# Attention and gated layer of four batches on one core: unit orders replaced, eleven zero products removed, first-batch products reordered, down projection in two units a bank

## The reference

```
xn = layernorm(x)
s  = causal_attention(xn; 16 heads of 16) @ Wo.T
W  = (wq - 128) * scale[:, None]            # for gate, up and down
g  = silu( (silu(xn @ Wgate.T) * (xn @ Wup.T)) @ Wdown.T )   # hidden size 704
out = x + s * g
```

## Time and profile before

| what | value |
|---|---|
| median of 3 runs | 287.1 us (285.98 to 288.08) |
| the profiled execution's own time | 287.32 us |
| its span, first to last instruction | 285.6 us |
| mean granted TensorE clock | 0.994 |
| PE busy | 272.3 us, 95% of the span |
| PEld / DVE / ACT / POOL busy | 202.0 / 209.5 / 174.0 / 133.1 us |

### The profile page before, as it was taken

How to read it: one execution, slowest core, us unless ns; L and a number is a source line. 1 busy time by engine, 2 the same in 40 slices (tenths; PEclk the granted TensorE clock), 3 DMA queues, 4 the chain that set the end, 5 groups by cost and what they waited for, 6 DMA issues and landing times.

```text
span 285.6 us, 5873 instructions
## 1 busy us (share of the span) xinstructions
PE 272.3 (95%) x2088; PEld 202.0 (71%) x2088; DVE 209.5 (73%) x722; ACT 174.0 (61%) x258; POOL 133.1 (47%) x235
## 2 busy tenths in 40 slices
...
GB/s 266 328 165 203 182 5 2 76 3 112 187 220 9 3 0 6 76 182 153 190 6 6 0 2 3 37 42 137 158 158 77 2 3 2 148 3 3 2 2 73
DMA packets 18005, 23.11 MB, mean 81 GB/s; under 512 B 2936, under 2 KB 11064, under 8 KB 17976
## 3 DMA queue, kind: packets, MB, share of 16 engines
...
...
## 4 chain that ended last, share of the span: by engine, by line
PE 73%; DVE 17%; issue 2%; POOL 2%; DMA 2%; SPq 2%; ACT 1%; ACTq 1%; DVEq 0%
PE ps L428 15%; PE ps L430 12%; PE ps L429 12%; PE ps L578 12%; DVE ps L1007 10%; PE ps L561 8%; PE ps L543 6%; PE ps L588 3%; DMA tailt<-in_su 2%; DVE mx L1007 2%; PE ps L597 1%; PE ps L472 1%; DVE cn L1018 1%; POOL kp L809 1%; DVE hid L986 1%
## 5 line engine op out<-in xcount | busy, mean ns | idle before, releaser
L1007 DVE CUSTOM_DVE_ANT_0 ps<-ps,maskt 128x512 f32<-128x512 f32 (+3 forms) x256 | 117.5, 523 | 16.2 <-PE ps L543 15.7
L854 POOL TENSOR_SCALAR_AFFINE_SELECT pt<-pt 128x256 f32<-128x256 f32 (+1 forms) x112 | 47.7, 442 | 88.2 <-ACT pt L781 87.2
L781 ACT ACTIVATE pt<-ps 128x1024 f32<-128x1024 f32 x80 | 79.4, 1025 | 9.9 <-PE ps L561 8.3
L830 POOL TENSOR_TENSOR hid<-hid 128x512 f32<-128x512 f32 x24 | 32.0, 1333 | 18.4 <-DVE hid L986 9.4
L578 PE MATMUL ps<-pt,vt 128*32 128x256 f32 (+3 forms) x528 | 39.2, 439 | 0.3 <-DVE mx L1007 0.2
L428 PE MATMUL ps<-xh,guh 128*128 128x512 f32 x88 | 37.8, 430 | 1.1 <-DVE xr L979 0.4
L1007 DVE DVE_READ_ACCUMULATOR2_ANT mx<- 128x1 f32 x256 | 36.0, 141 | 0.0
L543 PE MATMUL ps<-kp,qp 64*128 64x512 f32 (+3 forms) x256 | 32.9, 342 | 2.0 <-DVE mx L1007 1.8
L430 PE MATMUL ps<-xh,gul 128*128 128x512 f32 x88 | 34.6, 393 | 0.0
L429 PE MATMUL ps<-xl,guh 128*128 128x512 f32 x88 | 34.5, 392 | 0.0
L561 PE MATMUL ps<-qp,kp 64*128 64x512 f32 (+3 forms) x256 | 33.1, 344 | 0.2 <-DVE mx L1007 0.2
...
## 6 DMA issues: line engine op xcount, KB each, us to landing
...
```

The source lines that it names most:

```text
L781: nc.scalar.activation(pair(b, s), ps[:, b0:b1 + 1:b1 - b0, :], ACT.Exp, scale=SCALE).then_inc(exp_done, 1)
L830: nc.gpsimd.tensor_tensor(a, a, hid[:, m % 2, 1, :], ALU.mult).then_inc(h_done, 1)
L854: mm = nc.gpsimd.affine_select(out=diag, in_=diag, compare_op=ALU.is_ge, fill=0.0, base=0, pattern=[[0, diag.shape[1]], [1, P]], channel_m ...
L1007: mm = nc.vector.tensor_tensor_reduce(part, part, maskt[:, T - wide:], -1.0, TOP, ALU.add, ALU.min, mg[:, e, a // 2, i:i + 1])
```

## The change

- All five order texts are replaced, with other banks. The numbers of units are the same, but for the next point but two.
- `WARM` goes from 36 to 29 and `FILL` is removed, with the zero products in `qk:0:0`.
- In batch 0 the six matmuls of every `qk` and `gu` unit come from a new function `first_split`: high weights times the high part of `x`, high weights times its low part, and low weights last; each group waits only for its own operands. `transpose_x` waits for its four `xn` tiles one by one.
- `dn` becomes two units: `da` takes the bank and does the first tile of 128 tokens, `dn` the second tile in the same bank.

The diff, cut to the lines that are spoken of (order texts: heads and ends):

```diff
-WARM = 36
-FILL = 4
+WARM = 29
 TENSOR_ORDER = """
-t:0:0:0 t:0:1:1 qk:0:0:0 qk:0:1:1 qk:0:2:2 gu:0:0:0 gu:0:1:1 qk:0:3:2 m:0:0:01 m:0:1:34 m:0:2:56 gu:0:2:7 gu:0:3:2
-gu:0:4:0 gu:0:5:7 m:0:3:12 m:0:4:34 gu:0:6:0 gu:0:7:1 gu:0:8:2 m:0:5:01 m:0:6:34 c:0:0:5 gu:0:9:6 v:0:0:0 v:0:1:1
-s:0:0:56 s:0:1:23 m:0:7:07 gu:0:10:4 s:0:2:01 m:0:8:56 s:0:3:23 m:0:9:57 s:0:4:01 m:0:10:26 m:0:11:35 m:0:12:01
...
+t:0:0:0 t:0:1:1 qk:0:0:2 qk:0:1:0 qk:0:2:1 gu:0:0:3 gu:0:1:2 gu:0:2:4 gu:0:3:2 gu:0:4:5 gu:0:5:2 gu:0:6:0 m:0:0:13
+m:0:1:46 qk:0:3:7 gu:0:7:1 gu:0:8:3 m:0:2:24 m:0:3:56 gu:0:9:7 gu:0:10:0 m:0:4:14 v:0:0:2 v:0:1:1 m:0:5:34 m:0:6:56
+t:1:0:0 c:0:0:2 m:0:7:17 t:1:1:3 m:0:8:45 da:0:0:2 dn:0:0 da:0:1:3 m:0:9:01 s:0:0:45 s:0:1:67 dn:0:1 m:0:10:02
+s:0:2:45 s:0:3:67 qk:1:0:1 c:0:1:0 s:0:4:34 m:0:11:25 m:0:12:06 gu:1:0:7 m:0:13:23 pv:0:0:4 m:0:14:02 s:0:5:56
...
-z2:3:0:0 dn:3:0:7 s:3:15:01 pv:3:2:2 s:3:16:01 s:3:17:34 s:3:18:56 zt:3:2:2 oa:3:0:7 s:3:19:01 dn:3:1:2 pv:3:3:0
-pv:3:4:1 zt:3:3:0 oa:3:1:2 zt:3:4:1 z2:3:1:0 z2:3:2:1 o:3:0 o:3:1
+da:3:0:4 c:3:3:0 zt:3:1:1 dn:3:0 pv:3:2:0 s:3:15:12 s:3:16:34 s:3:17:56 z2:3:0:0 da:3:1:7 zt:3:2:1 s:3:18:23
+s:3:19:45 dn:3:1 pv:3:3:0 pv:3:4:1 zt:3:3:0 oa:3:0:2 zt:3:4:1 z2:3:1:0 oa:3:1:3 z2:3:2:1 o:3:0 o:3:1
 SCALAR_ORDER = """
-init:0:0 whi:0:0 whi:0:1 whi:0:2 ghi:0:0 ghi:0:1 xhi:0:0 xhi:0:1 woh:0:0 qhi:0:0 pkah:0:0 pkal:0:0 qhi:0:1 qhi:0:2
...
+init:0:0 whi:0:0 whi:0:1 whi:0:2 ghi:0:0 xhi:0:0 xhi:0:1 ghi:0:1 qhi:0:0 pkah:0:0 qhi:0:1 woh:0:0 qhi:0:2 pkal:0:0
+tanh:0:0 up:0:0 tanh:0:1 up:0:1 wdh:0:0 xn:1:0 xn:1:1 xn:1:2 xn:1:3 hhi:0:0 hhi:0:1 qhi:0:3 tanh:0:2 up:0:2 tanh:0:3
 VECTOR_ORDER = """
-init2:0:0 st:0:0 xn:0:0 wlo:0:0 xn:0:1 xn:0:2 xn:0:3 wlo:0:1 wlo:0:2 xlo:0:0 xlo:0:1 glo:0:0 glo:0:1 qlo:0:0 wds:0:0
-qlo:0:1 qlo:0:2 wol:0:0 gate:0:0 wdl:0:0 qlo:0:3 maxa:0:0 maxb:0:0 gate:0:1 maxa:0:1 maxb:0:1 maxa:0:2 gate:0:2
...
+init2:0:0 st:0:0 xn:0:0 xn:0:1 xn:0:2 xn:0:3 wlo:0:0 wlo:0:1 xlo:0:0 xlo:0:1 glo:0:0 glo:0:1 qlo:0:0 bn:1:0 bn:1:1
+bn:1:2 bn:1:3 mom:1:0 wol:0:0 wds:0:0 qlo:0:1 qlo:0:2 gate:0:0 gate:0:1 wdl:0:0 maxa:0:0 maxb:0:0 maxa:0:1 maxb:0:1
+qlo:0:3 gate:0:2 wlo:0:2 gate:0:3 maxa:0:2 maxb:0:2 maxa:0:3 maxb:0:3 maxa:0:4 gate:0:4 maxb:0:4 gate:0:5 sh:0:0
+maxa:0:5 maxb:0:5 maxa:0:6 hlt:0:0 xlo:1:0 maxb:0:6 maxa:0:7 xlo:1:1 maxb:0:7 maxa:0:8 maxb:0:8 u:0:0 bn:2:0 bn:2:1
 SYNC_ORDER = """
-init4:0:0 loadx:1:0 pkh:0:0 pkl:0:0 pkh:0:1 pkh:0:2 pkh:0:3 pkl:0:1 pkl:0:2 pkl:0:3 loadres:0:0 crow:0:0 crow:0:1
...
+init4:0:0 loadx:1:0 pkh:0:0 pkh:0:1 pkh:0:2 pkl:0:0 pkl:0:1 pkl:0:2 loadx:2:0 pkh:0:3 pkl:0:3 loadres:0:0 crow:0:0
...
             def transpose_x(b, k):
                 bank, = take(("t", b, k))
-                if k == 0:
-                    w.need("xn", xn_done, TT * (b + 1))
                 for i in range(TT):
+                    w.need("xn", xn_done, TT * b + i + 1)
...
+            def first_split(dst, hi, lo, cols, hi_name, hi_sem, lo_name, lo_sem, part):
+                w.need(hi_name, hi_sem, part)
+                for k in range(KD):
+                    w.need("xhi", xhi_done, k + 1)
+                    nc.tensor.matmul(dst, hi[:, k, cols], xh[:, k, :], start=k == 0, stop=False)
+                for k in range(KD):
+                    w.need("xlo", xlo_done, k + 1)
+                    nc.tensor.matmul(dst, hi[:, k, cols], xl[:, k, :], start=False, stop=False)
+                w.need(lo_name, lo_sem, part)
+                for k in range(KD):
+                    mm = nc.tensor.matmul(dst, lo[:, k, cols], xh[:, k, :], start=False, stop=k == KD - 1)
+                return mm
...
+            def down_first(b, n):
+                bank, = take(("da", b, n))
                 w.need("hlo", hlo_done, HF * (b + 1))
                 w.need("hlt", hlt_done, b + 1)
                 w.need("wdl", wdl_done, 1)
+                down_tile(2 * n, bank)
+
+            def down_rest(b, n):
+                down_tile(2 * n + 1, bank_of("da", b, n)).then_inc(f_ready, 1)
```

More of the change, by code:

```diff
@@ L74 @@
[L74 to L78, removed]
@@ L97 @@
[L97 to L101, removed]
@@ L102 @@
[L102 to L106, removed]
@@ new lines @@
+maxb:0:15 maxa:0:16 maxb:0:16 maxa:0:17 maxb:0:17 maxa:0:18 maxb:0:18 gate:1:1 qlo:1:2 maxa:0:19 maxb:0:19 sh:0:3
+maxa:1:0 maxb:1:0 bn:3:3 norm:0:1 mom:3:0 maxa:1:1 maxb:1:1 zlo:0:0 gate:1:2 qlo:1:3 maxa:1:2 maxb:1:2 maxa:1:3
+maxb:1:3 maxa:1:4 maxb:1:4 maxa:1:5 maxb:1:5 sh:1:0 gate:1:3 norm:0:2 maxa:1:6 maxb:1:6 maxa:1:7 maxb:1:7 maxa:1:8
+maxb:1:8 gate:1:4 maxa:1:9 maxb:1:9 maxa:1:10 maxb:1:10 sh:1:1 norm:0:3 zlo:0:1 gate:1:5 xlo:2:0 xlo:2:1 fin:0:0
+fin:0:1 qlo:2:0 hlt:1:0 qlo:2:1 gate:2:0 maxa:1:11 maxb:1:11 maxa:1:12 maxb:1:12 maxa:1:13 maxb:1:13 u:1:0 maxa:1:14
@@ new lines @@
+maxb:2:15 gate:2:5 maxa:2:16 xlo:3:0 xlo:3:1 maxb:2:16 hlt:2:0 maxa:2:17 maxb:2:17 maxa:2:18 maxb:2:18 maxa:2:19
+maxb:2:19 sh:2:3 qlo:3:0 u:2:0 qlo:3:1 u:2:1 norm:2:1 gate:3:0 qlo:3:2 zlo:2:0 qlo:3:3 maxa:3:0 maxb:3:0 maxa:3:1
+maxb:3:1 maxa:3:2 maxb:3:2 maxa:3:3 maxb:3:3 maxa:3:4 maxb:3:4 gate:3:1 maxa:3:5 maxb:3:5 sh:3:0 gate:3:2 norm:2:2
+maxa:3:6 maxb:3:6 maxa:3:7 maxb:3:7 maxa:3:8 maxb:3:8 maxa:3:9 norm:2:3 gate:3:3 maxb:3:9 sh:3:1 maxa:3:10 maxb:3:10
+zlo:2:1 maxa:3:11 maxb:3:11 maxa:3:12 maxb:3:12 maxa:3:13 maxb:3:13 maxa:3:14 gate:3:4 maxb:3:14 sh:3:2 maxa:3:15
@@ L131 @@
+mask:3:12 mask:3:13 mask:3:14 mask:3:15 mask:3:16 mask:3:17 mask:3:18 mask:3:19
 """
 SYNC_ORDER = """
-init4:0:0 loadx:1:0 pkh:0:0 pkl:0:0 pkh:0:1 pkh:0:2 pkh:0:3 pkl:0:1 pkl:0:2 pkl:0:3 loadres:0:0 crow:0:0 crow:0:1
-loadx:2:0 crow:0:2 pkh:1:0 pkl:1:0 pkh:1:1 pkl:1:1 pkh:1:2 pkh:1:3 crow:0:3 loadx:3:0 pkl:1:2 pkl:1:3 crow:1:0
-crow:1:1 sout:0:0 sout:0:1 pkh:2:0 pkl:2:0 pkl:2:1 pkh:2:1 pkh:2:2 crow:1:2 loadres:1:0 pkl:2:2 pkh:2:3 pkl:2:3
-crow:1:3 crow:2:0 crow:2:1 sout:1:0 crow:2:2 sout:1:1 loadres:2:0 pkh:3:0 pkh:3:1 pkl:3:0 pkl:3:1 crow:2:3 pkh:3:2
@@ L137 @@
-pkl:3:2 pkh:3:3 pkl:3:3 crow:3:0 crow:3:1 sout:2:0 crow:3:2 sout:2:1 loadres:3:0 crow:3:3 sout:3:0 sout:3:1
+init4:0:0 loadx:1:0 pkh:0:0 pkh:0:1 pkh:0:2 pkl:0:0 pkl:0:1 pkl:0:2 loadx:2:0 pkh:0:3 pkl:0:3 loadres:0:0 crow:0:0
+crow:0:1 pkh:1:0 loadx:3:0 pkl:1:0 pkh:1:1 pkl:1:1 crow:0:2 pkh:1:2 pkl:1:2 crow:0:3 pkh:1:3 pkl:1:3 crow:1:0
+sout:0:0 pkh:2:0 sout:0:1 pkh:2:1 loadres:1:0 crow:1:1 pkl:2:0 pkl:2:1 crow:1:2 crow:1:3 pkh:2:2 pkl:2:2 crow:2:0
+pkh:2:3 pkl:2:3 crow:2:1 sout:1:0 crow:2:2 sout:1:1 loadres:2:0 pkh:3:0 pkl:3:0 pkh:3:1 pkl:3:1 crow:2:3 pkh:3:2
@@ L138 @@
+pkl:3:2 pkl:3:3 pkh:3:3 crow:3:0 crow:3:1 crow:3:2 sout:2:0 sout:2:1 crow:3:3 loadres:3:0 sout:3:0 sout:3:1
 """
@@ L509, in gate_up @@
                 bank, = take(("gu", b, n))
-                w.need("xlo", xlo_done, KD * (b + 1))
-                w.need("gul", gul_done, 1 if n % 2 == 0 else 2)
                 at = (n // 2 if n % 2 == 0 else HF + 1 + n // 2) * P
                 cols = slice(at, at + P)
+                if b == 0:
+                    first_split(ps[:, bank, :], guh, gul, cols, "guh", guh_done, "gul", gul_done, n % 2 + 1
+                                ).then_inc(gu_ready, 1)
+                    return
+                w.need("xlo", xlo_done, KD * (b + 1))
                 for k in range(KD):
@@ L517, in gate_up @@
                 mm.then_inc(gu_ready, 1)
-            def down(b, n):
-                bank, = take(("dn", b, n))
+            def down_first(b, n):
+                bank, = take(("da", b, n))
                 w.need("hlo", hlo_done, HF * (b + 1))
@@ L523, in down, with down_tile @@
                 w.need("wdl", wdl_done, 1)
-                for i in (2 * n, 2 * n + 1):
-                    rows = slice(i * P, (i + 1) * P)
-                    dst = ps[:, bank, (i % 2) * D:(i % 2 + 1) * D]
-                    for m in range(HF):
-                        split3(dst, hh[:, m, rows], hl[:, m, rows], wdh[:, m, :], wdl[:, m, :], m == 0, False)
-                    nc.tensor.matmul(dst, hh[:, HF, rows], wdh[:, HF, :], start=False, stop=False)
-                    mm = nc.tensor.matmul(dst, hh[:, HF, rows], wdl[:, HF, :], start=False, stop=True)
-                mm.then_inc(f_ready, 1)
+                down_tile(2 * n, bank)
+            def down_rest(b, n):
+                down_tile(2 * n + 1, bank_of("da", b, n)).then_inc(f_ready, 1)
+            def down_tile(i, bank):
+                rows = slice(i * P, (i + 1) * P)
+                dst = ps[:, bank, (i % 2) * D:(i % 2 + 1) * D]
+                for m in range(HF):
+                    split3(dst, hh[:, m, rows], hl[:, m, rows], wdh[:, m, :], wdl[:, m, :], m == 0, False)
+                nc.tensor.matmul(dst, hh[:, HF, rows], wdh[:, HF, :], start=False, stop=False)
+                return nc.tensor.matmul(dst, hh[:, HF, rows], wdl[:, HF, :], start=False, stop=True)
             def maxima(b, m):
```

139 lines of the change are left out of this document (65 added, 74 removed).

## The result

The changed kernel takes **275.6 us** (median of four runs, 274.97 to 276.03) against 287.6 for the kernel before in the same series: a ratio of 0.959, 95% interval 0.954 to 0.964. The forecast was 280.8, the range 277.0 to 287.5: the sign and most mechanisms came as forecast, the size was nearly twice the forecast. The profiled execution took 274.97 us, span 273.2.

The account below looks back on a forecast made before the run. It took TensorE's own work, plus what stands before, between and after it, as the bound (PE busy 95%). Sum: 287.3 - 2.5 - 1.3 - 1.4 - 2.4 - 0.6 + 1.7 = 280.8 us; range 277 to 287.5.

Parts of the forecast that it names:

- The rest: Two more waits a batch in three batches, of some 0.28 us, from longer runs of one kind: 1.7 us charged.
- My lower bound, -1.6: Low end of the charge for more bank waits: today's waits vanish, -1.6 us.
- 0.08: Chance left for better than the forecast: 1.7 us charge not needed, more first-batch waits gone, 277 us.
- First batch: TensorE's waits up to `qk:1:0`: 2.5 us where 3.8 stood, gain 1.3 us.
- Clock: No fall to the 1.2 GHz level after the first batch's waits, in the first `pv` unit: gain 1.4 us.
- Switches: Full-array units meeting half-row or `pv` units on TensorE: 122 before, 98 after, 0.1 us each, gain 2.4 us.
- Head: Fourteen zero instructions fewer and earlier operands: `qk:0:1` starts near 13.2 against 15.73, gain 2.5 us.
- Tail: `oa:3:0` moves into the gap after the second last `z2`: gain 0.6 us.
- VectorE didn't set the pace of the first batch: Rival: VectorE paces the first batch, the earlier PE start turns into waits: 285.5 us, chance 0.2.
- the first maximum: Sign in the first batch: VectorE meets its first maximum at 26 to 27.
- No stall spread to the later batches: Rival: first-batch stall and clock fall in each of three batches, 15.6 us: 296.4 us, chance 0.1.
- The clock stayed at 1.00 through the thin stretch of transposes: Rival: the clock falls at the head after transposes, price 1.4 to 1.7 us: 282.4 us, chance 0.1.

Follow-up runs that it names:

- Run 3: The changed kernel with each `dn` put right behind its `da`, so the down projection is whole in all batches: 281.69 us, ratio 0.9774.
- Run 4: The changed kernel with the down projection of batch 0 and its consumers moved behind `pv:0:0`: 283.72 us, ratio 0.9859.
- run 12: The changed kernel with the old order of the six matmuls in batch 0, all operands awaited at the unit's head: 277.15 us, ratio 0.9647.
- run 9: The changed kernel itself, unaltered, run again in the next series: 275.99 us, ratio 0.9592.
- run 5: The changed kernel plus full-array and half-row zero products alternating 1 by 1, 2 by 2, 4 by 4: blocks of 13.83, 10.62 and 9.03 us.
- run 1: The kernel before with its own orders and whole down units, plus only the new head (`WARM` 29, no `FILL`, `first_split`, waits tile by tile): 286.51 us, ratio 0.9965.
- runs 2: The changed kernel with `WARM` back at 36, `FILL` still out: 276.52 us, ratio 0.9604.

## Why the prediction was wrong

- **"The rest", +1.7 us, is the step that failed most:** -2.2 was measured, 3.9 us off. I argued that longer runs of one kind make a wait for a bank likelier, and no row bore that. Run 3 shows what I left out: the second down unit is a filler that can be put off to a gap in any batch, and without the cut the waits behind `pv:0:0` are 3.6 us longer. My lower bound, -1.6, was wrong too: I took it from missing busy time, where the starts show 11.5 us, some 4 of it in pieces over 0.15. How much the old orders, or new ones for whole units, would keep was not tried, nor were the new bank numbers tried apart from the orders. The prediction gave 0.08 to what came, that the 1.7 isn't needed and more of the first batch's waits go, and put it outside the range.
- **First batch, -1.3; measured -3.5.** The places were right (`c:0:0` 0.5, `m:0:8` 0.8, `da:0:0` 0.4), but the six I listed came to three, with a fourth, `pv:0:0` 0.7, that I hadn't; and the waits of before, 3.8 in the idle column, are 6.4 by starts. I had also taken a down tile for 14 matmuls where it has 17: 8.2 us of filler, not 6.7. Run 4 shows that the filler is what removed them.
- **Clock, -1.4:** right for the two profiled executions, in size too; run 4 brings the fall back. My reason, more and shorter waits, isn't shown: run 12 fell after the same waits with which run 9 didn't.
- **Switches, -2.4; -2.7:** right by two errors that cancel. The 24 meetings that go are right (16 of full-array with half-row units, 8 with `pv`). But the earlier trace rows shows only the full-array unit's share; the half-row unit pays as much again (run 5). And eight meetings of half-row with `pv` units come, which I took as free and which cost the half-row side 0.1. By the count 16 x 0.2 + 8 x 0.1 - 8 x 0.1 = 3.2, by the starts 2.7.
- **Head, -2.5; -1.8.** The zero products ran 0.144 us apart on average (6.04 by 42), not 0.112, since they stood 0.21 apart until 7.2 us, against 5.5 us in the trace before; so the transposes began at 10.56 and not at 9.8. Other executions have `qk:0:1` at 13.3, where I put it. Why the zero products are slow for longer in some is open. Worth by itself: about 1 us in the old orders, some 0.3 of it without a fall of the clock (run 1); in the new ones nothing shown (runs 2, 9).
- **Tail, -0.6; -0.8:** right.
- **The rivals.** VectorE didn't set the pace of the first batch; the first maximum came at 26.85, as forecast. No stall spread to the later batches. The clock stayed at 1.00 through the thin stretch of transposes, where in run 1, with a wait of 2.11 us behind them, it fell; no run tells the transposes' share in that from the wait's. So what the Trainium skill, "TensorE: Matmul & The Clock Gate", Part 4, says of transposes cost nothing in the changed kernel, and may have cost run 1 its lead.
